# The shared expert's units leave their sequence's stage; attention writes into the sum

## The chip, the cores and the metric
The kernel runs on one core of a Trainium2 chip. The metric is the time of one execution on the device in microseconds (us), median of the runs. Engines: PE (TensorE), DVE (VectorE), ACT (ScalarE), POOL (GpSimd), SP (SyncE, which here only issues transfers). Each runs its own queue in order; the queues meet through semaphores that the code sets and waits for by hand.

## The reference, cut to what matters
Eight sequences of 512 tokens, width 512, go through attention (softmax attention and a gated linear attention over the same projections; output added to the input by the kernel, "x2"), and then through a mixture of experts:

```
shared = (silu(x @ shared_gate.T) * (x @ shared_up.T)) @ shared_down.T    # 512 -> 512 -> 512, every token
topk_idx, topk_w = _router(x, router_w, e_bias)                           # 4 of 32 experts for each token
G, U = x[slots] @ W_gate[e], x[slots] @ W_up[e]                           # 160 slots an expert, 512 -> 256
out[slots_token] += (silu(G) * U) @ W_down[e] * slots_w
result = out + shared
```

The kernel is a pre-norm block, so a layer norm stands ahead of the router and both kinds of expert, and the sum starts from x2.

## The kernel before, in words
Three phases with a barrier between them: `attention_phase` (to 2157 us of the span), `routing_phase` (L1032, to 2552 us) and `expert_phase` (L1633). Products that need more than 16 bits are made of three fp16 products of a high and a low part (`THREE`).

**Routing.** One stage for each sequence b. It holds the whole shared expert for that sequence and the routing. The shared expert has eight units: four `gate_up(b, f)` (24 matmuls of 512 columns, L1391), here called G0 to G3, and four `down(b, i, ...)` (12 such matmuls, L1398), here D0 to D3. Behind each G, ACT takes the sigmoid, DVE makes two products (`silu_product`, L1566 and L1571), ACT rounds to the high part (`h_high`, L1293), POOL subtracts the low part (`h_low`, L1202). Behind each D, DVE adds the result onto x2 (`residual`, L1579), and SP stores the sum to `acc` (L1179). PE's order in a stage: G0, `turn(b+1)` (transposes of the next sequence, L1354), `places(b)` (L1373 to L1376, prefix sums for the slots), G1, `logits(b+1)` (L1363), G2, G3, D0 to D3. DVE's order: `placing(b)`, product 0, `slots(b)` (L1553 to L1560), `statistics(b+2)`, product 1, `refine(b+2)`, `group_scores(b+1)`, `best_groups(b+1)`, product 2, `picks(b+1)`, product 3, `count_picks(b+1)`, residuals. POOL's order: `y_low(b+1)`, `copy_tokens`, then 16 scatters of 128 rows of 2112 bytes into the table `rows` (L1217) with the four `h_low` between them. `slots(b)` waits for all 16 scatters of sequence b-1 to have landed, since they read the indices that it overwrites. SP loads x2 into three buffers `xr`, and at b = 5 the weights of the first `SETS` = 5 experts.

**Experts.** One iteration for each of 32 experts. PE: `gate_up(e)` (48 matmuls of 160 columns, L1872), `turn(e+1)` (8 transposes, L1859), `down(e-1)` (12 matmuls of 512 columns, L1885). ACT and DVE split each expert's weights into high and low parts, ACT copies the result out (`copy_down`, L1785). POOL computes each slot's weight and row (`weigh`, L1726 to L1735) and adds the result to `acc` in memory with two accumulating indirect transfers of 80 rows (`add`, L1744). `add(e)` waits until `add(e-1)` has landed, as two experts may hold the same token. Results wait in four buffers `yo`. At the end SP and ACT copy `acc` to the output (L1693).

Of the kernel before, what the change touches and what calls it, by code (L numbers as in the profile page):

```python
# [6 lines left out]
P = 128  # L7
# [9 lines left out]
DM = 512  # L17
# [974 lines left out]
SETS = 5  # L992


class Held:


    def __init__(self, nc, ctx, cap):
# [7 lines left out]
        self.own = sb("own", [ct, n_ct, E_])  # L1006
        self.up_loaded = [ctx.enter_context(nc.semaphore(f"expert_up_loaded{n}")) for n in range(SETS)]
        self.down_loaded = [ctx.enter_context(nc.semaphore(f"expert_down_loaded{n}")) for n in range(SETS)]

# [14 lines left out]
def load_expert(eng, held, w_gate, w_up, w_down, e):  # L1024
# [3 lines left out]
    eng.dma_start(held.up(n), w_up[e].rearrange("(p c) i -> p c i", p=P)).then_inc(held.up_loaded[n], 16)  # L1028
    eng.dma_start(held.down(n), w_down[e].rearrange("(p c) d -> p c d", p=P)).then_inc(held.down_loaded[n], 16)


def routing_phase(nc, x2, router_w, e_bias, shared_gate, shared_up, shared_down, consts, acc_dram, rows_dram, held,  # L1032
# [10 lines left out]
    with ExitStack() as ctx:  # L1043
# [19 lines left out]
        turned_w = [[sb(f"w_t{n}_{part}", [P, 4, DM], FP16) for part in ("high", "low")] for n in range(3)]  # L1063
        sg, su, sd = turned_w
        xr = [sb(f"xr{n}", [P, NT, DM]) for n in range(RING)]
# [5 lines left out]
        y_part = [[sb(f"y{n}_{part}", [P, DC, SEQ], FP16) for part in ("high", "low")] for n in range(2)]  # L1071
# [47 lines left out]
        x_loaded = [sem(f"x_loaded{n}") for n in range(RING)]  # L1119
# [29 lines left out]
        ONE_SCATTER = 16 * NT * K  # L1149

# [3 lines left out]
        def _(sp):  # L1154
            def load_x(b):
                sp.dma_start(xr[b % RING][:], x2[b].rearrange("(i p) d -> p i d", p=P)).then_inc(x_loaded[b % RING], 16)
# [13 lines left out]
            for b in range(1, min(RING, B)):  # L1170
                load_x(b)

            for b in range(B):
                if b == max(B - 3, 0):
                    sp.wait_ge(w_ready, 12)
                    for e in range(SETS):
                        load_expert(sp, held, w_gate, w_up, w_down, e)
                sp.wait_ge(summed, NT * (b + 1))
                sp.dma_start(acc_dram[b * SEQ:(b + 1) * SEQ, :].rearrange("(i p) d -> p i d", p=P), xr[b % RING][:]).then_inc(base_stored, 16)  # L1179
                if b + RING < B:  # L1180
                    sp.wait_ge(base_stored, 16 * (b + 1))
                    load_x(b + RING)
            sp.wait_ge(base_stored, 16 * B)

        @block.gpsimd
        def _(pool):
            pool.wait_ge(loaded, ALL_LOADS)

            def y_low(b):
                for i in range(NT):  # L1190
                    t = slice(i * P, (i + 1) * P)
                    if b >= 2:
                        pool.wait_ge(up_done, SC * (b - 1))
                    pool.wait_ge(y_high_ready, NT * b + i + 1)
                    nc.gpsimd.tensor_tensor(y_part[b % 2][1][:, :, t], y_t[:, :, t], y_part[b % 2][0][:, :, t],
# [28 lines left out]
            for b in range(B):  # L1224
# [14 lines left out]
        def _(act):  # L1239
# [8 lines left out]
            def norm(b):  # L1248
                act.wait_ge(newton_step, 9 * (b + 1))
                act.wait_ge(x_loaded[b % RING], 16 * (b // RING + 1))  # L1250
# [3 lines left out]
                for i in range(NT):  # L1254
                    nc.scalar.activation(yn[b % RING][:, i, 0:DM], xr[b % RING][:, i, :], ACT.Identity,
# [14 lines left out]
            def features(b):  # L1270
                for i in range(NT):
# [6 lines left out]
                    if b >= 2:  # L1278
                        act.wait_ge(up_done, SC * (b - 1))
                    nc.scalar.activation(y_part[b % 2][0][:, :, i * P:(i + 1) * P], turned, ACT.Copy, scale=X_SCALE).then_inc(y_high_ready, 1)  # L1280
# [27 lines left out]
            if B > 1:  # L1308
                norm(1)
            for b in range(B):  # L1310
                gate_sigmoid(b, 0)
                if b + 1 < B:
                    features(b + 1)
                h_high(b, 0)
                gate_sigmoid(b, 1)
# [4 lines left out]
                h_high(b, 1)  # L1320
# [4 lines left out]
                gate_sigmoid(b, 2)  # L1325
                h_high(b, 2)
                gate_sigmoid(b, 3)
                h_high(b, 3)

        @block.tensor  # L1330
        def _(pe):
# [47 lines left out]
            def gate_up(b, f):  # L1379
# [8 lines left out]
                for w, ps, done in ((sg, gate_ps, gate_done), (su, up_ps, up_done)):  # L1388
                    for d in range(DC):
                        for n, (y_, w_) in enumerate(THREE):  # L1390
                            ins = nc.tensor.matmul(ps[f % 2][:], w[w_][:, d, f * P:(f + 1) * P], y_part[b % 2][y_][:, d, :],  # L1391
# [13 lines left out]
            pe.wait_ge(w_ready, 12)  # L1405
            for b in range(B):
                gate_up(b, 0)
# [4 lines left out]
                gate_up(b, 1)  # L1412
# [4 lines left out]
                gate_up(b, 2)  # L1417
                gate_up(b, 3)
                pe.wait_ge(h_low_ready, SC * b + 3)
                pe.wait_ge(h_step, 2 * (SC * b + 2) + 1)  # L1420
                down(b, 0, (0, 1, 2))
                pe.wait_ge(h_step, 2 * (SC * b + 3) + 1)
                down(b, 1, (0, 1, 2))
                pe.wait_ge(h_low_ready, SC * (b + 1))
                down(b, 0, (3,))
                down(b, 1, (3,))
                for i in (2, 3):
                    pe.wait_ge(summed, NT * b + i - 1)
                    down(b, i, (0, 1, 2, 3))

        @block.vector
        def _(dve):
            def statistics(b):
                base = (2 * NT + 1) * b
                dve.wait_ge(x_loaded[b % RING], 16 * (b // RING + 1))
                for i in range(NT):
                    nc.vector.bn_stats(bn[:, i, :], xr[b % RING][:, i, :]).then_inc(stats_step, 1)
# [136 lines left out]
            def residual(b, i):  # L1574
                if i == 0:
                    dve.wait_ge(x_loaded[b % RING], 16 * (b // RING + 1))
                    dve.wait_ge(yn_ready, NT * (b + 1))
                dve.wait_ge(down_done, NT * b + i + 1)
                nc.vector.scalar_tensor_tensor(out=xr[b % RING][:, i, :], in0=down_ps[i % 2][:], scalar=1.0 / (O_SCALE * W_SCALE),  # L1579
                                               in1=xr[b % RING][:, i, :], op0=ALU.mult, op1=ALU.add).then_inc(summed, 1)  # L1580
# [22 lines left out]
            for b in range(B):  # L1603
                if b:
                    placing(b)
                silu_product(b, 0)
# [7 lines left out]
                silu_product(b, 1)  # L1614
# [8 lines left out]
                silu_product(b, 2)  # L1623
                if b + 1 < B:
                    picks(b + 1)
                silu_product(b, 3)
                if b + 1 < B:
                    count_picks(b + 1)
                for i in range(NT):
                    residual(b, i)  # L1630


def expert_phase(nc, T, w, rows_dram, acc_dram, out, held):  # L1633
# [7 lines left out]
    with ExitStack() as ctx:  # L1641
# [24 lines left out]
        tr_ps, gate_ps, up_ps, down_ps = banks("tr_ps"), banks("gate_ps"), banks("up_ps"), banks("down_ps")  # L1666
# [21 lines left out]
        yo_ready = sem("yo_ready")  # L1688
        ONE_ADD = 16 * n_ct

# [8 lines left out]
        def _(sp):  # L1699
# [6 lines left out]
            for e in range(XS):  # L1706
                load_x(e)
            for e in range(XS, E_):
                if e + 1 >= SETS and e + 1 < E_:
                    sp.wait_ge(w_low, 3 * (e + 1 - SETS + 1))  # L1710
# [269 lines left out]
```

## Time and profile before
| | |
|---|---|
| median of 3 runs | 2868.56 us (2867.84 to 2871.44) |
| the profiled execution's own time | 2872.15 us |
| its span | 2869.7 us |
| PE busy | 2592.1 us, 90% |
| DVE, ACT, POOL busy | 67%, 54%, 54% |
| routing phase, by the first issues of each phase on SP | 2161 to 2552 us |
| expert phase | 2552.5 us to the end |

Busy shares are over the whole span. A matmul's record is longer than its place in the queue, since matmuls overlap: what one costs is read from start to start.

### The profile page before, as it was taken

The numbers are of one execution on the slowest core, as the hardware profiler recorded it, in microseconds if no ns is written. First come the engines' busy times: TensorE is split into PE (matmuls) and PEld (weight loads), VectorE is DVE, ScalarE is ACT, GpSimd is POOL, SyncE is SP. The second block draws the span as 40 slices with busy tenths as digits, with TensorE's granted clock in tenths as the row PEclk, the third lists the DMA queues.
The fourth block names the chain that finished last, engine by engine and source line by source line (L and its number), as shares of the span: only waits on it lengthen the run. The fifth ranks groups of instructions, "written<-read, shape, count | busy, mean of one in ns | idle before, by whom it ended". The sixth has DMA issues, their size and how long they took to land. (4 is left out here: it accounts for less than half of the span.)

```text
span 2869.7 us, 52448 instructions
## 1 busy us (share of the span) xinstructions
PE 2592.1 (90%) x16740; PEld 1703.5 (59%) x16740; DVE 1936.6 (67%) x4731; ACT 1554.0 (54%) x4655; POOL 1549.3 (54%) x1623
## 2 busy tenths in 40 slices
PE   3899999999999999999999999999984899979882
PEld 2566666666666666666666666666653444447661
DVE  5677667677776776777677767767754777747661
ACT  4566556655655555666566555656543333237661
POOL 3556445655655564566556545655520566646663
PEclk9899999999999999999999999999996999989996
DMA  4500000000000000000000000000002222339985
GB/s 169 186 1 16 1 30 1 16 30 1 1 16 31 1 16 28 3 1 16 30 1 2 15 31 1 1 31 1 1 1 107 94 69 68 132 117 272 265 231 147
DMA packets 65355, 156.78 MB, mean 55 GB/s; under 512 B 13367, under 2 KB 14647, under 8 KB 64256
## 3 DMA queue, kind: packets, MB, share of 16 engines
q1 hardware_dynamic: 48624, 132.91, 13.6%
q0 software_dynamic: 16384, 16.33, 3.1%
q10 hardware_dynamic: 80, 4.19, 0.4%
q8 instruction: 141, 2.31, 0.3%
q14 instruction: 126, 1.03, 0.1%
HBM read 120.31 MB, written 81.40 MB: 70 GB/s over the span
## 5 line engine op out<-in xcount | busy, mean ns | idle before, releaser
L403 ACT ACTIVATE prob<-score_ps,neg_max 128x512 f32<-128x512 f32 (+3 forms) x512 | 271.8, 531 | 308.1 <-DVE neg_max L566 278.6
L280 POOL TENSOR_TENSOR parts<-qk,rope 128x640 f32<-128x640 f32 x128 | 197.0, 1539 | 383.1 <-issue 326.2
L793 PE MATMUL out_ps<-prob_t,val 128*128 128x512 f32 (+3 forms) x1024 | 302.3, 438 | 14.0 <-ACT prob_t L409 13.1
L768 PE MATMUL score_ps<-kr_t,qr_t 128*128 128x512 f16 (+3 forms) x1536 | 284.7, 300 | 13.0 <-ACT prob L403 11.2
L574 DVE TENSOR_SCALAR prob<-prob,inv_sum 128x512 f32<-128x512 f32 (+3 forms) x512 | 273.7, 535 | 18.0
L793 PEld LDWEIGHTS out_ps<-prob_t,val 128*128 128x128 f32 x1024 | 185.4, 191 | 127.6 <-issue 62.1
L445 ACT ACTIVATE soft<-qk,neg_top 128x128 f32<-128x128 f32 x640 | 247.1, 387 | 5.5 <-DVE neg_top L588 2.1
L566 DVE TENSOR_REDUCE neg_max<-score_ps 128x1 f32<-128x512 f32 (+3 forms) x512 | 237.4, 483 | 7.1 <-PE score_ps L770 0.9
L309 POOL TENSOR_TENSOR decay<-keys 128x512 f32<-128x512 f32 x128 | 134.0, 1047 | 167.0 <-DVE keys L616 167.0
L835 PE MATMUL qkv_ps<-wq_high,x_t_high 128*128 128x512 f16 x512 | 195.8, 382 | 15.8 <-DVE wkv_low L514 15.8
L318 POOL TENSOR_TENSOR k_dec<-decay,keys 128x512 f32<-128x512 f32 x128 | 163.0, 1273 | 68.7 <-ACT decay L461 68.7
L572 DVE RECIPROCAL inv_sum<-row_sum 128x1 f32<-128x1 f32 x512 | 81.4, 159 | 174.6 <-ACT prob L403 174.5
L292 POOL TENSOR_TENSOR rot<-parts 128x320 f32<-128x320 f32 x128 | 110.6, 864 | 162.9 <-DVE parts L596 162.9
L835 PE MATMUL qkv_ps<-wq_low,x_t_high 128*128 128x512 f16 x512 | 195.8, 382 | 0.0
L835 PE MATMUL qkv_ps<-wq_high,x_t_low 128*128 128x512 f16 x512 | 195.3, 381 | 0.0
L331 POOL TENSOR_TENSOR o_t_low<-parts,o_t_high 128x512 f16<-128x512 f32 x128 | 147.9, 1156 | 81.0 <-ACT parts L419 81.0
L768 PEld LDWEIGHTS score_ps<-kr_t,qr_t 128*128 128x128 f16 x1536 | 135.7, 98 | 82.8 <-ACT prob L403 38.3
L889 PE MATMUL tr_ps<-q_dec,k_dec 128*32 128x128 f32 (+3 forms) x1024 | 177.6, 293 | 5.0 <-POOL k_dec L318 2.9
L298 POOL TENSOR_TENSOR soft<-soft,inv_tot 128x512 f32<-128x512 f32 x128 | 145.4, 1136 | 60.5 <-DVE inv_tot L608 60.5
L409 ACT COPY prob_t<-prob_ps 128x384 f32<-128x384 f32 (+1 forms) x256 | 94.2, 368 | 141.4 <-DVE prob_t L582 137.1
L1744 POOL DMA_INDIRECT acc<-e_yo,e_goal x64 | 113.8, 1779 | 103.5 <-issue 85.2
L1217 POOL DMA_INDIRECT rows<-r_yn,r_sk_i x128 | 129.0, 1008 | 53.9 <-issue 47.3
(267 smaller groups left out, 7701.0 us busy)
## 6 DMA issues: line engine op xcount, KB each, us to landing
held_expert_w<-in_L_ffn_W_gate_dram SPq DMA_DIRECT2D x32, 512.0 KB
held_expert_w<-in_L_ffn_W_up_dram SPq DMA_DIRECT2D x32, 512.0 KB
held_expert_w<-in_L_ffn_W_down_dram SPq DMA_DIRECT2D x32, 512.0 KB, 7.7
rows<-const_empty_dram SPq DMA_DIRECT2D x1, 10560.0 KB, 38.8
e_xg<-rows SPq DMA_DIRECT2D x32, 330.0 KB
x_in<-_attn_hidden_states_dram SPq DMA_DIRECT2D x8, 1024.0 KB, 5.5
x_acc<-_attn_hidden_states_dram SPq DMA_DIRECT2D x8, 1024.0 KB, 5.5
x<-x_acc SPq DMA_DIRECT2D x8, 1024.0 KB, 4.4
```

The lines of the kernel that those rows point to most:

```text
L280: nc.gpsimd.tensor_tensor(parts[:, 1, :].rearrange("p (h d) -> p h d", d=HALF), qk[:].rearrange("p (h d) -> p h d", d=HALF), rope[:, i, 1: ...
L298: nc.gpsimd.tensor_tensor(q, q, inv_tot[:, 0:G].unsqueeze(2).to_broadcast([P, G, DH]), ALU.mult).then_inc(soft_query_ready, 1)
L318: nc.gpsimd.tensor_tensor(k_dec[:], decay[:, 0:NSUB * P].rearrange("p (c s) -> p c s", s=P), keys[:, 0:P].unsqueeze(1).to_broadcast([P, NS ...
L331: nc.gpsimd.tensor_tensor(o_t[1][:, h, :], o_whole, o_t[0][:, h, :], ALU.subtract).then_inc(o_t_ready, 1)
L403: nc.scalar.activation(prob[:, i % 2, 0:w], score_ps[i % 2][:, 0:w], ACT.Exp, bias=neg_max[:, j:j + 1], accum_out=row_sum[:, j:j + 1]).the ...
L445: ins = nc.scalar.activation(soft[:, h * DH:(h + 1) * DH], qk[:, h * DH:(h + 1) * DH], ACT.Exp, bias=neg_top[:, h:h + 1], accum_out=tot[:, ...
L566: nc.vector.tensor_reduce(neg_max[:, j:j + 1], score_ps[i % 2][:, 0:w], AX_X, ALU.max, negate=True).then_inc(max_ready, 1)
L574: nc.vector.tensor_scalar(prob[:, i % 2, 0:w], prob[:, i % 2, 0:w], inv_sum[:, j:j + 1], None, ALU.mult).then_inc(prob_ready, 1)
L768: nc.tensor.matmul(score_ps[i % 2][:, 0:w], qr_t[p][:, q_, h, i * P:(i + 1) * P], kr_t[p][:, k_, 0:w], start=(n == 0), stop=False)
L793: nc.tensor.matmul(out_ps[:, j * P:SEQ], val[p][:, j, :], prob_t[:, j, j * P:SEQ], start=(j == 0), stop=False, skip_group_check=True)
L835: ins = nc.tensor.matmul(qkv_ps[:, 0:G * DH], x_t[x_part][:, d, i * P:(i + 1) * P], wq[w][:, d, gn * G * DH:(gn + 1) * G * DH], start=(d = ...
L889: ins = nc.tensor.matmul(tr_ps[0][0:m, :].rearrange("p (h t) -> p h t", t=P)[:, :, m - SUB:m], k_dec[:, s, 0:m], q_dec[:, :, m - SUB:m], s ...
```

## The change
- The 64 units of the shared expert form one row, sequence after sequence. The first five sequences' 40 units are done during routing, five in each of the eight stages (`place`), whatever sequence they belong to. The remaining 24 units (three sequences: 12 G, 12 D) are done between the experts (`late_pieces`): one unit ahead of `gate_up(e)` in experts 0, 1, 2, 4, 5, 6, 8 and so on to 30, none in every fourth expert.
- To that end the normalised sequences stay in five buffers (`Y_RING`) and the shared weights stay in SBUF; preloaded expert weights go down from five sets to four; `xr` from three buffers to two. A separate buffer `x_sum` with its own loads serves the five early sequences.
- Attention writes x2 into the rows of `acc` itself. So the three late sequences need no base: their unit results are added to `acc` by four accumulating indirect transfers of 128 rows per sequence on POOL (`s_add`), with a wait for the adds before and a wait of the next `add` for them.
- Expert phase: `gate_ps` and `up_ps` go from two banks to one each (two banks go to the late units), the order of ACT, DVE and POOL within an iteration changes, weights are loaded in two steps.

```diff
-SETS = 5
+SETS = 4
+EARLY = 5
+PIECES = 2 * 4
+Y_RING = 5
...
+        IN_STAGE = EARLY * PIECES // B
+        def place(b, n):
+            q = IN_STAGE * b + n
+            return q // PIECES, q % PIECES
...
-                h_low(b, 0)
-                scatter(b, range(0, 3))
-                h_low(b, 1)
-                scatter(b, range(3, 9))
-                h_low(b, 2)
-                scatter(b, range(9, 10))
-                h_low(b, 3)
-                scatter(b, range(10, NT * K))
+                for n, some in enumerate((range(0, 3), range(3, 8), range(8, 10), range(10, 12), range(12, NT * K))):
+                    q, part = place(b, n)
+                    if part < SC:
+                        h_low(q, part)
+                    scatter(b, some)
...
+            def piece(b, n):
+                q, part = place(b, n)
+                if part < SC:
+                    gate_up(q, part)
+                else:
+                    i = part - SC
+                    pe.wait_ge(h_low_ready, SC * (q + 1))
+                    if i >= 2:
+                        pe.wait_ge(summed, NT * q + i - 1)
+                    down(q, i, range(SC))
...
+            def s_add(q, experts):
+                pool.wait_ge(added, ONE_ADD * experts)
+                pool.wait_ge(s_out_ready, NT * (q + 1))
+                for i in range(NT):
+                    n = NT * (EARLY + q) + i
+                    pool.indirect_dma_start(acc_dram, bass.IndirectOffsetOnAxis(ap=held.token_i[:, n:n + 1], axis=0), s_out[:, i, :], None,
                                            bounds_check=T + cap - 1, oob_is_err=True, compute_op=ALU.add).then_inc(s_added, 16)
...
             for e in range(E_):
-                if e + 2 < E_:
-                    weigh(e + 2)
-                add(e)
+                for q, part in late_pieces(e):
+                    if part < SC:
+                        s_low(q, part)
+                if e:
+                    if e + 1 < E_:
+                        weigh(e + 1)
+                    add(e - 1)
+                for q, part in late_pieces(e):
+                    if part == PIECES - 1:
+                        s_add(q, e)
+            add(E_ - 1)
...
-                if e >= 2:
-                    pe.wait_ge(h_step, 2 * (e - 1))
+                if e:
+                    pe.wait_ge(h_step, 2 * e)
...
-            turn(0)
             for e in range(E_):
+                for q, part in late_pieces(e):
+                    s_piece(q, part)
+                if not e:
+                    turn(0)
                 gate_up(e)
...
-    x2 = scratch("x2", [B, SEQ, DM])
-    acc = scratch("acc", [B * SEQ + cap, DM])
+    acc = scratch("acc", [T + cap, DM])
+    x2 = acc[0:T, :].rearrange("(b t) d -> b t d", b=B)
```

## Rows read from the trace of the kernel before
**Rows 1.** Windows: length, busy us (instructions) of each engine, granted clock, DMA share, GB/s
```profile
2300.00:2400.00 100.00, 94.49 (x515) 48.72 (x513) 70.27 (x177) 34.72 (x61) 63.28 (x62) 0.98 0.22 72
2700.00:2800.00 100.00, 83.60 (x779) 65.97 (x777) 67.57 (x95) 64.35 (x107) 61.78 (x94) 0.98 0.87 239
```
**Rows 2.** Timeline, PE, one routing stage: start, duration, instruction
```profile
2352.99 0.27 PE L1354 MATMUL r_tr_ps<-held_ident,r_yn 128*128 128x128 f32 x1
2356.31 0.18 PE L1373 MATMUL r_pos_ps<-r_picked_b,r_before_b 128*128 128x32 bf16 x1
2356.66 0.38 PE L1391 MATMUL r_gate_ps<-r_y_high,r_w_t_high 128*128 128x512 f16 x1
2361.84 0.19 PE L1363 MATMUL r_lg_ps<-r_rw_t,r_y_t 128*128 128x32 f32 x1
2365.69 0.61 PE L1391 MATMUL r_gate_ps<-r_y_high,r_w_t_high 128*128 128x512 f16 x1
...
2377.36 0.38 PE L1398 MATMUL r_gate_ps<-r_w_t_high,r_h_high 128*128 128x512 f16 x1
2388.13 0.38 PE L1391 MATMUL r_gate_ps<-r_y_high,r_w_t_high 128*128 128x512 f16 x1
```
**Rows 3.** Timeline, DVE, the same stage
```profile
2356.85 0.29 DVE L1553 TENSOR_SCALAR r_over<-r_pos_ps 128x128 f32<-128x128 f32 x1 [2.91 <-PE r_pos_ps L1376]
...
2372.52 0.69 DVE L1566 TENSOR_TENSOR r_sig<-r_sig,r_gate_ps 128x512 f32<-128x512 f32 x1
...
2377.63 0.69 DVE L1566 TENSOR_TENSOR r_sig<-r_sig,r_gate_ps 128x512 f32<-128x512 f32 x1
...
2378.95 1.05 DVE L1525 TENSOR_REDUCE r_picked<-r_hot 128x128 f32<-128x512 f32 x1
...
2381.61 0.19 DVE L1473 TENSOR_TENSOR r_seen<-r_seen,r_seen_now 128x32 f32<-128x32 f32 x1
```
**Rows 4.** Timeline, DVE: one cast, for sequences 1 and 4
```profile
2248.45 0.23 DVE L1516 CAST r_at_f<-r_at 128x32 f32<-128x32 uint32 x1
...
2375.13 1.74 DVE L1516 CAST r_at_f<-r_at 128x32 f32<-128x32 uint32 x1
```
**Rows 5.** Timeline, DVE and POOL: `slots(1)`, its first and last scatter, first of sequence 7
```profile
2276.59 0.29 DVE L1553 TENSOR_SCALAR r_over<-r_pos_ps 128x128 f32<-128x128 f32 x1 [2.91 <-PE r_pos_ps L1376]
...
2281.76 1.02 POOL L1217 DMA_INDIRECT rows<-r_yn,r_sk_i  x1 [0.90 <-DVE r_sk_i L1560]
...
2307.29 0.97 POOL L1217 DMA_INDIRECT rows<-r_yn,r_sk_i  x1 [0.31 <-issue]
...
2516.98 1.00 POOL L1217 DMA_INDIRECT rows<-r_yn,r_sk_i  x1 [0.90 <-DVE r_sk_i L1560]
```
**Rows 6.** Timeline, SP: first transfers of the expert phase
```profile
2552.46 1.80 SPq L1704 DMA_DIRECT2D e_xg<-rows  x4
```
**Rows 7.** Timeline, PE, and a window: D units of sequence 7 after a wait
```profile
2533.23 0.61 PE L1398 MATMUL r_gate_ps<-r_w_t_high,r_h_high 128*128 128x512 f16 x1 [4.51 <-POOL r_h_low L1202]
...
2530.00:2540.00 10.00, 6.77 (x19) 2.53 (x20) 0.00 (x0) 0.15 (x1) 8.40 (x9) 0.66 0.03 4
```
**Rows 8.** Timeline, PE: first matmuls of two experts early in the phase
```profile
2580.28 0.23 PE L1872 MATMUL e_gate_ps<-e_xp_t_high,e_wg_high 128*128 128x160 f16 x1
...
2587.16 0.23 PE L1872 MATMUL e_gate_ps<-e_xp_t_high,e_wg_high 128*128 128x160 f16 x1
```
**Rows 9.** View of line L1744: all adds, then landing from issue
```profile
L1744 POOL DMA_INDIRECT acc<-e_yo,e_goal x64: 1414/1708/2516, 2575.2 to 2838.1; - x64
...
DMA to landing us min/median/max: 3.9/5.9/8.8
```
**Rows 10.** Timeline, POOL and SP: last adds and the copy to the output
```profile
2836.34 1.41 POOL L1744 DMA_INDIRECT acc<-e_yo,e_goal  x1 [3.30 <-issue]
2838.06 1.42 POOL L1744 DMA_INDIRECT acc<-e_yo,e_goal  x1 [0.30 <-issue]
...
2842.00 0.55 SPq L1693 DMA_DIRECT2D out_dram<-acc  x1
```

More of the change, by code:

```diff
@@ L1070, in routing_phase @@
         y_t = sb("y_t", [P, DC, SEQ])
-        y_part = [[sb(f"y{n}_{part}", [P, DC, SEQ], FP16) for part in ("high", "low")] for n in range(2)]
+        y_part = held.y_part
+        x_sum = sb("x_sum", [P, NT, DM])
         bn = sb("bn", [P, NT, 6])
@@ L1118, in routing_phase @@
         w_ready = sem("w_ready")
-        x_loaded = [sem(f"x_loaded{n}") for n in range(RING)]
+        x_loaded = [sem(f"x_loaded{n}") for n in range(2)]
+        x_sum_loaded = sem("x_sum_loaded")
         gate_done = sem("gate_done")
@@ L1324, in _ @@
                     norm(b + 2)
[L1325 to L1328, printed above, removed]
+                for n in range(2, IN_STAGE):
+                    sigmoid_of(b, n)
+                    high_of(b, n)
         @block.tensor
@@ L1416, in _ @@
                     logits(b + 1)
[L1417 to L1429, printed above, removed]
+                for n in range(2, IN_STAGE):
+                    piece(b, n)
         @block.vector
@@ L1572, in silu_product, with residual, piece @@
                                                in1=up_ps[f % 2][:], op0=ALU.mult, op1=ALU.mult).then_inc(h_step, 1)
-            def residual(b, i):
+            def residual(q, i):
                 if i == 0:
[L1576 to L1580, printed above, removed]
+                    dve.wait_ge(x_sum_loaded, 16 * (q + 1))
+                dve.wait_ge(down_done, NT * q + i + 1)
+                nc.vector.scalar_tensor_tensor(out=x_sum[:, i, :], in0=down_ps[i % 2][:], scalar=1.0 / (O_SCALE * W_SCALE),
+                                               in1=x_sum[:, i, :], op0=ALU.mult, op1=ALU.add).then_inc(summed, 1)
+            def piece(b, n):
+                q, part = place(b, n)
+                if part < SC:
+                    silu_product(q, part)
+                else:
+                    residual(q, part - SC)
             statistics(0)
@@ L1622, in _ @@
                     best_groups(b + 1)
[L1623 removed]
+                piece(b, 2)
                 if b + 1 < B:
                     picks(b + 1)
[L1626 removed]
+                piece(b, 3)
                 if b + 1 < B:
                     count_picks(b + 1)
[L1629 to L1630 removed]
+                for n in range(4, IN_STAGE):
+                    piece(b, n)
 def expert_phase(nc, T, w, rows_dram, acc_dram, out, held):
@@ L1665, in expert_phase @@
         h_part = [[sb(f"h{n}_{part}", [P, FC, cap], FP16) for part in ("high", "low")] for n in range(2)]
-        tr_ps, gate_ps, up_ps, down_ps = banks("tr_ps"), banks("gate_ps"), banks("up_ps"), banks("down_ps")
+        tr_ps, down_ps = banks("tr_ps"), banks("down_ps")
+        gate_ps, up_ps, wide_ps, wider_ps = (ctx.enter_context(nc.psum_tensor(f"e_{name}", [P, 512], F32))
+                                            for name in ("gate_ps", "up_ps", "wide_ps", "wider_ps"))
+        s_sig = sb("s_sig", [P, SEQ])
+        s_h = sb("s_h", [P, SEQ])
+        s_part = [sb(f"s_{part}", [P, SC, SEQ], FP16) for part in ("high", "low")]
+        s_out = sb("s_out", [P, NT, DM])
+        sg, su, sd = held.shared_w
         def by_chunk(bank):
```

233 lines of the change are left out of this document (180 added, 53 removed).

## The prediction
> **What bounds the kernel now.** I read the windows by stretch first. In routing PE is busy 94 of 100 us with DMA at 0.22; among the experts PE has 84 of 100 and DMA 0.87 [rows 1]. So the two phases have different limits, and the change moves PE work from the one where PE is full to the one where it isn't.
>
> In routing the timeline of PE shows a stage of 40.1 us without gaps (first scatter of sequence 1 to that of sequence 7: 2516.98 - 2281.76 = 235.2 us, six stages, of which the last is shorter, 34.2; the other five take 40.1 to 40.3) [rows 5]. From start to start a G costs 5.2 us (2356.66 to 2361.84), four D cost 10.8 (2377.36 to 2388.13), so 2.7 each, the transposes 3.3, the places 0.35, the logits 3.85 [rows 2]. 4 x 5.2 + 10.8 + 7.5 = 39.1; a wait of 1.2 us inside G2 makes up the rest. PE sets the stage.
>
> Among the experts PE takes 6.9 us for one when nothing holds it (2580.28 to 2587.16) [rows 8], but 64 adds in 32 pairs start from 2575.2 to 2838.1, 263 / 31.5 = 8.3 us a pair [rows 9]. A pair needs 1.7 us from the first issue to the second, and then the landing, for which the next pair waits: 4.7 us at the quiet end (3.30 idle + 1.42), median 5.9 [rows 9, 10]. 1.7 + 5.9 and the hand-over are some 8 us: the chain of adds on POOL sets this phase, and PE loses 1.4 us an expert.
>
> **Routing after the change.** Its PE work per stage falls from 39.1 to (20 x 5.2 + 20 x 2.7) / 8 + 7.5 = 27.2 us. By that alone the eight stages would give back 95 us. They can't: another chain lies close below. `slots(b)` on DVE waits for all scatters of b-1. From its start S to the first scatter it is 5.2 us (2276.59 to 2281.76); sixteen scatters stand 1.28 us apart (with four `h_low` between them 25.5 us from first to last: 15 x 1.28 + 3 x 1.2 and two short waits) [rows 5]; then the last must land. For the landing of a scatter no row exists. The nearest are the adds: 3.9 us at the least, 5.9 median, from the issue [rows 9]. A plain write should not be slower than a read and write; I take 4.0, with 2.5 and 5.9 as ends. So POOL's chain without waits is 5.2 + 19.2 + 4.0 = 28.4 us, and 1.3 for each `h_low` between.
>
> The second limit is DVE's order. From S: to the end of `best_groups` 15.7 us with a G product inside (2356.85 to 2372.52), 15.0 with a residual (0.7 for 1.3); then unit 2 and `picks` 5.1 (4.5 with a residual; 2372.52 to 2377.63), unit 3 1.3 or 0.7, `count_picks` 2.85 (2378.95 to 2381.8), unit 4 [rows 3]. If unit 4 is a G, its product ends at S + 24 to 26, then ACT's rounding and POOL's `h_low` take 2.0, and only then come the last four scatters (3.85) and the landing. The stages, with their five units:
> - stage 0 (G G G G D): starts as before; its D0 waits for the fourth `h_low` at 2257 (three scatters more than before stand ahead of it, but only one D follows, not four). `slots(1)` at 2268.9, against 2276.6: 7.7 earlier.
> - stage 1 (D D D G G): unit 4 ends at 24.9; + 2.0 + 3.85 + 4.0 = 34.7.
> - stage 2 (G G D D D): 28.4 + 2.1 for an `h_low` that waits = 30.5.
> - stage 3 (D G G G G): unit 4 at 26.3, `h_low` at 28.3; PE's D0 of the same sequence waits for it, then transposes and places: + 4.9 + 3.7 = 37.0.
> - stage 4 (D D D D G): 24.2 + 2.0 + 7.85 = 34.0, and 1 more as the experts' weights load just then.
> - stage 5 (G G G D D): D0 waits for G3's `h_low` at 19.1; D0, D1, D2 (4.9 + 2.6 + 2.6), transposes and places 3.8 = 33.1.
> - stage 6 (D D G G G): no `statistics`; POOL 28.4 + 3 x 1.3 and hand-overs = 32.8.
> The D behind a wait is taken at 4.9, not 2.7: a D after 4.5 us of waiting starts at 0.61 us a matmul, and the window has a granted clock of 0.66, so partly 1.2 and not 2.4 GHz [rows 7].
> From stages 1 and 4 I take off 2.0 and 2.5: DVE's cast took 1.74 us where an `h_low` ran on POOL beside it and 0.23 where none did [rows 4], and these stages have fewer `h_low` in that place. Sum: 32.7 + 30.5 + 37.0 + 32.5 + 33.1 + 32.8 = 198.6, so `slots(7)` at 2467.5. Sixteen scatters, landing and barrier, 28.3 more: the expert phase starts at 2495.8, where it started at 2552.5 [rows 6]. **Gain 56.7 us.** (Bounds: with landings of 5.9 us the five stages that end on one and the phase's end give 11 back; with 2.5, 9 more are gained.)
>
> SP's new waits cost nothing: the loads of x2 for the norm and of `x_sum` are issued at least 5 us ahead of their reader in each stage by the same chain; the latest is sequence 7's, issued at the end of stage 4, needed 13 us later. If that cover were gone, each late load would cost its 5.6 us once. Preloading four sets instead of five is hidden too: the fifth is asked for as soon as expert 0's weights are split, four experts ahead. In attention the stores go to other addresses, the same number: nothing.
>
> **Experts after the change.** Here PE becomes the limit: 6.9 us an expert and 12 x 5.2 + 12 x 2.6 = 93.3 us for the late units, 314 in all, against 8.3 x 32 = 266 for the adds. Step by step from the phase's start: G0 cold takes 7.6 and hides the first loads, transposes and the split of x 2.3 (the first `gate_up` at 10.2); 31 iterations at 6.88, less the missing first `down`, 210.7; the other 23 units 88.1. PE ends iteration 30 at 309.0. ACT and DVE need some 6 us an expert plus 1.3 for a G, below PE's 6.9 plus 5.2; the single banks `gate_ps` and `up_ps` are free 0.7 us after `gate_up`, while PE transposes and runs `down` (3.6 us): nothing. If that cover went, each us would cost 31.
> `s_add` lengthens POOL's chain three times. An accumulating transfer of 128 rows isn't in the trace; by the 80-row ones (1.42 us and 0.3 between) four of them and a landing are 3 x 1.72 + 4.7 = 9.9; scaled with the rows 13.7; I take 11.5. The first two are absorbed: POOL needs 8 us an expert, PE 9.8 on average, and the four `yo` buffers hold the lag for the six experts in which it is caught up. The third lies in the last iteration, ahead of the last two adds: 0.9 + 6.5 (add 29) + 11.5 + 6.5 + 5.7 (1.7 + 3.9) = 31.1 [rows 10]. Then the copy to the output, 27.7 (2842.0 to 2869.7) [rows 10]. 309.0 + 31.1 + 27.7 = 367.8, against 317.2 before. **Loss 50.6 us** (bounds: 48 to 58 by the transfer's size and a cold or warm start).
>
> **Sum.** Span 2495.8 + 367.8 = 2863.6, 6.1 less than 2869.7. The profiled execution took 2872.15, 3.6 above the median of the runs; on the median the forecast is 2868.56 - 6.1 = 2862.5 us. Two sums of 50 us nearly cancel: PE's idle time in the experts was only 1.4 x 32 = 45 us, and half of it comes back as the tail.
>
> The Trainium skill (TensorE: Matmul & The Clock Gate, Part 1, "What's actually happening") says that the slow clock is the default state and activity releases it. That agrees with the window at 0.66 [rows 7], and speaks against the change, as routing now has PE waits in each stage: it is the first rival. The skill (DMA: Bandwidth & Descriptors, "Anatomy of one DMA") gives a transfer a fixed 2.0 us plus its bytes at 436 GB/s; for 270 KB that is an estimate of 2.6 us, near my lower end, and by it routing would gain 8 us more. No row shows it; a case near it is rival 3.
>
> **Rivals.**
> 1. *Routing waits cost more than I took.* PE waits 5 to 10 us in each stage and starts slow, not only in two: 2.5 us in each of four more, and scatters land in 5.9: 10 + 11 = 21, so the net is +15, 2883; with half of it 2873. For it: rows 7. Against: in most stages PE isn't last, so a slow start is hidden. It decides when PE's transposes end later than the landing.
> 2. *The adds' chain isn't absorbed (the other side).* If POOL lags beyond the four buffers after each `s_add`, or the loaded landing of the 128-row transfers is longer, ACT's `copy_down` holds PE's `down`: 2 x 11.5 = 23 more, net +17, 2885. For it: this very chain sets the phase now. Against: it must lag about 20 us before it reaches PE, and one `s_add` is 11.5.
> 3. *Routing goes better:* landings of 2.5 us and fewer stretched DVE operations in all stages, 2 us each: 9 + 8 = 17 more, 2846.
> 4. *The stage doesn't shorten* since DVE and POOL were as full as PE: then +50 - 10. Against: DVE has 70 of 100, POOL 63 [rows 1], and the sums above.
>
> **Chances.** My forecast with its own range of 2852 to 2870: 0.45 (of it faster 0.25, within 0.16, slower 0.04). Rival 1: 0.18 (slower 0.14, within 0.04). Rival 2: 0.13 (slower 0.12, within 0.01). Rival 3: 0.19, faster. Rival 4: 0.05, slower. About 0.2% (5.7 us) is what a measurement of this kernel can tell from no change. Faster 0.44, within 0.21, slower 0.35. The range 2846 to 2883 leaves out the far end of rivals 2 and 4.
>
> **What will show it.** First scatters of the sequences 30 to 37 us apart, with the longest behind the stage with four G; the experts' first loads near 2496 (over 2505: rival 1; under 2485: rival 3). Among the experts PE busy over 95 of 100, without waits for `e_xp_t_low`, DMA under 0.87; PE's `down` waiting for `e_yo` would be rival 2. The last add some 31 us behind PE's last but one expert. The forecast is wrong if the routing phase gains under 45 us or the expert phase loses over 60.

## The result and the profile after

The changed kernel takes 2881.6 us (median; 2878.5 to 2884.9) beside 2871.4 us of the kernel before in the same session, a ratio of 1.0037 (95% interval 1.0023 to 1.0052). It is 10 us slower; the forecast was 6 us faster. The profiled execution took 2881.60 us, and its span is 2879.7 us, 10.0 more than before.

First the rows of the page that answer to the table of before: the engines' busy times, the granted clock and the DMA share in 40 slices.

```profile
span 2879.7 us, 52505 instructions
...
PE 2596.8 (90%) x16740; PEld 1708.1 (59%) x16740; DVE 1921.5 (67%) x4719; ACT 1571.3 (55%) x4667; POOL 1580.5 (55%) x1636
...
PE   3899999999999999999999999999985788799892
...
PEclk9899999999999999999999999999996989899996
DMA  4500000000000000000000000000003314288876
```

PE's busy time is the same (2592.1 before), as the same work is done. To see where time went I cut the span at two issues on SP: the first load of routing (2163.82, before 2161.24) and the first load of the experts:

```profile
2494.10 1.32 SPq L1786 DMA_DIRECT2D e_xg<-rows  x3
```

Routing takes 330.3 us where it took 391.2 [rows 6], 60.9 less. The expert phase takes 385.6 (2879.7 - 2494.1) where it took 317.2, 68.4 more. Attention ends 2.6 later. 68.4 + 2.6 - 60.9 = 10.1. The forecast had 56.7 less and 50.6 more: routing was right within 4.2 us, and the expert phase was forecast 17.8 us too short.

The windows of the changed kernel, with the columns of rows 1: one in routing, one in the quiet middle of the expert phase, one behind it.

```profile
2300.00:2400.00 100.00, 82.55 (x453) 44.51 (x452) 73.34 (x220) 38.67 (x67) 72.51 (x72) 0.90 0.24 81
2620.00:2720.00 100.00, 100.00 (x826) 70.82 (x825) 64.58 (x89) 65.23 (x102) 67.24 (x85) 1.00 0.84 233
2720.00:2780.00 60.00, 48.15 (x377) 34.35 (x376) 28.75 (x38) 27.59 (x44) 38.16 (x47) 0.89 0.70 181
```

PE fell from 94 to 83 of 100 us in routing, and its granted clock from 0.98 to 0.90. In the expert phase it is busy, but for 1 us, from its first matmul up to 2727, as forecast. Then a hole opens. The view of waits of PE over the expert phase has three rows (total, times, longest), the first of which is the end of routing:

```profile
PE e_wide_ps L2052 <- PEq L1054: 16.9, 1, 16.9
PE e_gate_ps L2024 <- DVE e_xp_t_low L1949: 10.4, 2, 9.3
PE e_wide_ps L2063 <- POOL e_s_low L1843: 2.5, 1, 2.5
```

To find what stands behind the 9.3 us I read the timelines of the engines ahead of PE, each row with its idle time and releaser. PE waits for DVE's low part of x. But DVE itself had waited, and so had ACT, whose rounding of x comes behind its rounding of the late product (`s_high`):

```profile
2736.61 0.31 PE L2024 MATMUL e_gate_ps<-e_xp_t_high,e_wg_high 128*128 128x160 f16 x1 [9.34 <-DVE e_xp_t_low L1949]
```
```profile
2732.53 0.62 ACT L1912 CAST e_s_high<-e_s_h 128x512 f16<-128x512 f32 x1 [14.09 <-DVE e_s_h L1979]
```
```profile
2731.81 0.69 DVE L1979 SCALAR_TENSOR_TENSOR e_s_h<-e_s_sig,e_wider_ps 128x512 f32<-128x512 f32 x1 [11.87 <-POOL e_s_low L1843]
```

DVE can't write the next late G into the one buffer `s_h` before POOL has subtracted the low part (`s_low`) of the last. And POOL stands in `s_add`:

```profile
2712.28 2.47 POOL L1835 DMA_INDIRECT acc<-e_yo,e_goal  x1 [2.14 <-issue]
...
2723.33 1.58 POOL L1850 DMA_INDIRECT acc<-e_s_out,held_token_i  x1 [6.86 <-DMA acc<-e_yo,e_goal]
...
2728.93 1.55 POOL L1850 DMA_INDIRECT acc<-e_s_out,held_token_i  x1 [0.30 <-issue]
2729.94 1.73 POOL L1843 TENSOR_TENSOR e_s_low<-e_s_h,e_s_high 128x512 f16<-128x512 f32 x1
...
2735.53 1.59 POOL L1835 DMA_INDIRECT acc<-e_yo,e_goal  x1 [2.36 <-DMA acc<-e_s_out,held_token_i]
```

From the add before the second `s_add` to the add behind it, 23.3 us pass (2712.28 to 2735.53); the three steps ahead of it are 9.7, 8.6 and 7.9. The four instructions of `s_add` take 7.2 us to issue (2723.33 to 2730.48), and `s_low` comes behind them. Its input has been ready since 2709.8, where ACT's `s_high` ends, so only its place in the queue makes it wait.

PE feels the second `s_add` and not the first. Two things differ. Behind the first, expert 11, where the second G of the next sequence could stand, has no late unit, so that G comes an expert later; behind the second `s_add` it comes at once, in expert 22. And POOL was later: this is read from how far an expert's add starts behind the end of PE's product for it. Here are the last matmuls of two products; their adds are those at 2712.28 and 2735.53 above:

```profile
2702.77 0.38 PE L2037 MATMUL e_down_ps<-e_wd_high,e_h_low 128*80 128x512 f16 x1
...
2714.84 0.38 PE L2037 MATMUL e_down_ps<-e_wd_high,e_h_low 128*80 128x512 f16 x1
```

The distance goes from 9.1 to 20.3 us. Ahead of the first `s_add` it was 1.6; that one made it 14.1, and ten experts later it was still 9.1. So the second met a POOL that had not caught up with the first. Without these 7.5 us (9.1 - 1.6) PE's wait of 9.34 would be about 2, as an estimate.

PE has lost 9.34 + 2.51 us in waits, and 2.6 + 1.6 in the slow starts behind them (the gate and up products of that expert take 5.9 us instead of 3.3, at a granted clock of 0.62 from 2736 to 2744; the D behind the other wait 4.2 instead of 2.6, at 0.72 from 2772 to 2778). That is 16.1 of the 17.8 us. PE ends its last but one expert at +325.3 from the phase's start (2819.39), where +309.0 was forecast. The rest is in the tail: 32.2 us up to the copy instead of 31.1, and 28.1 for the copy instead of 27.7.

### The profile page after: what moved, and what is told of

Read it like the earlier page. It is cut to its first block and busy times, and to the rows that moved or that the text cites. A ratio compares the mean times of both kernels' runs of the same rounds, so it can differ in the third digit from the quotient of the medians.

```text
span 2879.7 us, 52505 instructions
## 1 busy us (share of the span) xinstructions
PE 2596.8 (90%) x16740; PEld 1708.1 (59%) x16740; DVE 1921.5 (67%) x4719; ACT 1571.3 (55%) x4667; POOL 1580.5 (55%) x1636
## 5 line engine op out<-in xcount | busy, mean ns | idle before, releaser
L793 PE MATMUL out_ps<-prob_t,val 128*128 128x512 f32 (+3 forms) x1024 | 302.4, 439 | 14.0 <-ACT prob_t L409 13.1
```

The source lines that it names most:

```text
L793: nc.tensor.matmul(out_ps[:, j * P:SEQ], val[p][:, j, :], prob_t[:, j, j * P:SEQ], start=(j == 0), stop=False, skip_group_check=True)
```

## The experiments

Each is compared with the kernel before on the same chip. Lengths of the phases are from one profiled execution of each kernel, which isn't always near the median: for e2 it took 2874.0 us, for e10 2886.5, for e11 2861.5.

| kernel | median us | ratio to before, interval | routing | experts |
|---|---|---|---|---|
| changed kernel | 2881.6 | 1.0037 [1.0023, 1.0052] | 330.3 | 385.6 |
| e1: two `s_h` | 2881.2 | 1.0031 [1.0020, 1.0041] | 330.3 | 386.2 |
| e2: `s_add` one turn later | 2879.9 | 1.0030 [1.0019, 1.0041] | 326.9 | 382.3 |
| e3: no `s_add` | 2849.5 | 0.9924 [0.9908, 0.9939] | 327.3 | 356.6 |
| e4: before, x2 in the sum | 2871.7 | 0.9997 [0.9989, 1.0006] | 388.2 | 317.4 |
| e8: `s_low` on DVE | 2870.5 | 0.9997 [0.9985, 1.0009] | 328.1 | 377.8 |
| e5: no late units | 2821.0 | 0.9826 [0.9804, 0.9848] | 326.8 | 326.1 |
| e13: e5 with two banks | 2818.3 | 0.9808 [0.9794, 0.9822] | 328.2 | 327.1 |
| e9: e8, six early | 2871.8 | 1.0002 [0.9991, 1.0014] | 348.7 | 357.3 |
| e10: e9, late units in front | 2871.5 | 1.0002 [0.9985, 1.0020] | 352.1 | 367.1 |
| e11: sum at the end | 2856.1 | 0.9933 [0.9920, 0.9946] | 330.3 | 362.2 |
| e12: e11, six early | 2854.0 | 0.9927 [0.9914, 0.9940] | 350.8 | 336.2 |

The kernels with the changed routing and five early sequences have 326.8 to 330.3 us of routing, so differences of 3 us between single profiles mean nothing.

**e1, two buffers for the late product.** The first theory blamed the single buffer.

```diff
-        s_h = sb("s_h", [P, SEQ])
+        s_h = [sb(f"s_h{n}", [P, SEQ]) for n in range(2)]
...
-                if m:
-                    dve.wait_ge(s_low_ready, m)
-                nc.vector.scalar_tensor_tensor(out=s_h[:], ...
+                if m >= 2:
+                    dve.wait_ge(s_low_ready, m - 1)
+                nc.vector.scalar_tensor_tensor(out=s_h[m % 2][:], ...
```

> The changed kernel with two s_h buffers instead of one: DVE's product of a late G waits for the s_low before the last, no longer for the last. Theory A (the stall of PE at 2727 to 2737 and at 2770 comes from s_low standing behind s_add(1) on POOL, which the single s_h hands to DVE, ACT and the split of x): the waits of 9.34 and 2.51 us and the slow starts behind them (2.6 and 1.6) go, 16 us less, 2865 to 2868 us median, expert phase 370. DVE's wait of 11.87 us for s_low is gone, but the s_low itself is still late: D0 of that sequence comes four units later, so nobody misses it. Rival B (the lag of the chain of adds behind s_add is what PE pays, through copy_down and yo or through the x split): the wait moves to another name and the time stays at 2879 to 2882. Rival C (the miss is in the routing or attention phase): no change either, and the expert phase stays 385.

Measured: 2881.2 us, no gain to be told from the changed kernel, and an expert phase of 386.2. PE's waits in it:

```profile
...
PE e_wide_ps L2063 <- POOL e_s_low L1843: 13.5, 1, 13.5
PE e_gate_ps L2024 <- DVE e_xp_t_low L1949: 1.1, 1, 1.1
```

The wait of 9.34 us has gone and one of 13.5 has come, three experts later, at the next sequence's D0, which needs all four `s_low`. So theory A fell: the buffer chooses the place of the stall and not its size. POOL is late, and whatever PE needs from it next shows that. This is rival B, but with `s_low` as the path, not `yo`.

**e2, `s_add` one turn later.**

```diff
-                for q, part in late_pieces(e):
-                    if part == PIECES - 1:
-                        s_add(q, e)
+                for o in (e - 1, e):
+                    for q, part in late_pieces(o):
+                        if part == PIECES - 1 and (o < e) == (o < 30):
+                            s_add(q, e)
...
```

> The changed kernel with the first two s_add moved one turn of POOL's loop later, so that the s_low of the next sequence's G0 stands ahead of s_add(1) and not behind it; the one s_h stays. Theory A (s_low behind s_add): the stall goes, 12 to 16 us less, 2866 to 2870. The next G1's s_low (one expert later) may now stand behind s_add(1) and leave up to 4 us of it. Rival B (the length of POOL's chain, wherever s_add stands): no change, 2880 to 2882, with the stall one expert later.

Measured: 2879.9, ratio 1.0030; again at most 2 us, where theory A wanted 12 to 16. PE's longest wait is for the same `s_low`, at D0:

```profile
...
PE e_wide_ps L2064 <- POOL e_s_low L1843: 9.7, 1, 9.7
PE e_gate_ps L2025 <- DVE e_xp_t_low L1950: 2.1, 2, 1.1
```

Rival B again: it is the lag of POOL's queue, not the place of one instruction in it.

**e3, no `s_add`.** The late results are computed and left out of the sum.

```diff
-                for q, part in late_pieces(e):
-                    if part == PIECES - 1:
-                        s_add(q, e)
...
```

> The changed kernel without any s_add: the three late sequences' shared results are computed and not added to the sum. Theory A: the whole stall goes (16 us) and the tail loses the third s_add (11.9 us by the profile after): 28 less, 2853 us, expert phase 357. If s_add cost only its tail (rival B, the stall has another cause): 12 less, 2870, and PE still waits about 9 us for e_xp_t_low near expert 21.

Measured: the expert phase is 356.6 us, 29.0 less than in the changed kernel (28 expected); the ratio went from 1.0037 to 0.9924, that is 32 us. PE has no wait in the phase over 1.1 us and ends its last but one expert at +307.6. The `s_add` calls cause the whole stall and 11 us of the tail (49.0 us behind that end instead of 60.3).

**e4, one part of the change alone: x2 in the rows of the sum.**

```diff
-    x2 = scratch("x2", [B, SEQ, DM])
-    acc = scratch("acc", [B * SEQ + cap, DM])
+    acc = scratch("acc", [T + cap, DM])
+    x2 = acc[0:T, :].rearrange("(b t) d -> b t d", b=B)
```

> The kernel before with one part of the change alone: attention writes x2 into the rows of the sum, everything else as it was. Theory A (same stores, other addresses): ratio 1.000, the first routing load at 2161 us. Rival (the phase of attention is 2.6 us longer in the changed kernel because of the place of its stores): 2.6 us more, 2874 on a median of 2871.4, first routing load at 2164.

Measured: 0.9997, first routing load at 2160.76. The stores' new place costs nothing. The 2.6 us by which attention ended later in the changed kernel's profile are chance: that load stands anywhere from 2160.65 to 2166.78 in the profiles of the kernels here.

**e8, `s_low` on DVE.** This cuts the path by which POOL's lag reached PE and leaves the lag.

```diff
...
                 down_low(e)
+                for q, part in late_pieces(e):
+                    if part < SC:
+                        s_low(q, part)        # now nc.vector.tensor_tensor
                 if e + 1 < E_:
                     x_low(e + 1)
```

> The changed kernel with the subtraction s_low of the late G units moved from POOL to DVE (behind the split of the third weight), one s_h as before: nothing that PE needs for a late unit stands behind an s_add any more. Theory A2 (POOL's lag behind s_add reaches PE only through s_low, wherever the buffer lets it out: 13.5 us of it in the run with two s_h): the waits of PE in the expert phase go, expert phase 385.6 - 16 - about 1 (twelve s_low of 1.66 us less in POOL's chain matter only in the tail) = 369, the ratio to before 0.998, 2867. Rival B2 (the lag reaches PE also through the slots' shares of `weigh`, for which ACT's copy_down already waited 3 us in that run, or through yo): PE then waits for e_yo instead, 8 to 12 us, and the ratio stays at 1.002 or more.

Measured: ratio 0.9997, 11 us better than the changed kernel by the ratios, about 8 by the phase's length, and level with the kernel before. The window where the hole was, and the waits of PE over the whole expert phase:

```profile
2720.00:2780.00 60.00, 60.00 (x496) 42.64 (x495) 39.45 (x59) 40.31 (x64) 37.11 (x49) 1.00 0.81 216
```
```profile
...
PE e_gate_ps L2024 <- DVE e_xp_t_low L1939: 1.1, 1, 1.1
```

PE now ends its last but one expert at 2797.61, +308.9: the 309.0 of the forecast. So the path was `s_low`. But the phase is 377.8 long and not 369. The missing 9 us are in the tail, in POOL's timeline:

```profile
2807.27 1.49 POOL L1835 DMA_INDIRECT acc<-e_yo,e_goal  x1 [1.74 <-issue]
...
2813.69 1.58 POOL L1843 DMA_INDIRECT acc<-e_s_out,held_token_i  x1 [3.21 <-DMA acc<-e_yo,e_goal]
...
2825.86 1.41 POOL L1835 DMA_INDIRECT acc<-e_yo,e_goal  x1 [5.03 <-DMA acc<-e_s_out,held_token_i]
...
2832.29 1.42 POOL L1835 DMA_INDIRECT acc<-e_yo,e_goal  x1 [3.30 <-issue]
```

The add of expert 29 starts at 2807.27, 9.7 us behind PE's product for it, where in the changed kernel it starts 1.6 behind (2821.01 against 2819.39). POOL hasn't caught up by the end: its distance behind PE was 1.6 us ahead of the first `s_add` and 14.3 behind it, 9.1 ahead of the second and 22.7 behind it, and 9.7 here. The adds' chain sets the end of the phase, with PE's waits gone. Half of the stall that was removed came back as lag in the tail.

**e5 and e13, no late units; and then two banks again.** Both leave the shared expert of the last three sequences out of the result. e5 gives the routing gain alone; e13 tests the forecast's "nothing" for the single banks.

```diff
-            return [(n // PIECES, n % PIECES) for n in range(3 * (e + 1) // 4, 3 * (e + 2) // 4) if n < LATE]
+            return []
...
```
```diff
...
-                for w_part, ps, done in ((wg_part, gate_ps, gate_done), (wu_part, up_ps, up_done)):
+                for w_part, ps, done in ((wg_part, (gate_ps, wide_ps)[e % 2], gate_done), (wu_part, (up_ps, wider_ps)[e % 2], up_done)):
```

> The changed kernel without any late unit in the expert phase: the shared part of the last three sequences is left out, routing is as in the changed kernel. It gives the routing gain alone. If the two phases are independent (theory): routing 330, expert phase set by the chain of adds again at 8.3 us an expert, 317; together 61 less than before, 2812, ratio 0.979. If the new order on POOL and ACT or the four sets of weights cost something by themselves (rival): expert phase 322 or longer, 2817 and more.

> The kernel without late units (the last three sequences' shared part left out) with two PSUM banks each for the experts' gate and up products again, as in the kernel before. The run without late units had an expert phase of 326.1 us against 317.2 before, with adds 8.7 us apart and not 8.4, and PE waiting 38.6 us for the low part of x. Theory D (memory traffic and the new order of loads): no change, 326. Rival E (the single banks cost something when PE isn't the limit): 317 to 320, 6 to 9 us less than the 2821 of that run.

Measured: e5 has 326.8 us of routing and 326.1 of experts, 2821.0 in all. Routing is as long as with late units, so the two phases are independent; the expert phase is 9 us longer than before, the rival's side (2817 and more) and not the theory's 2812. Nearly all of it lies between the first add and the last: 31 steps of 8.7 us instead of 8.4. e13 has 327.1 by its profile, so the banks don't make the 9 us; its ratio is 0.0018 lower than that of e5, with intervals that overlap. What does make them stays open. In e5's middle window the DMA share is higher than in rows 1 at the same bytes, which fits adds that come some 9.5 us apart there, but isn't shown as the cause:

```profile
2620.00:2720.00 100.00, 80.06 (x738) 65.26 (x739) 58.83 (x86) 59.07 (x96) 55.41 (x88) 0.95 0.95 239
```

**e9 and e10, six sequences early.** Both on the basis of e8.

```diff
-EARLY = 5
+EARLY = 6
...
+            return [divmod(e // 2, PIECES)] if e % 2 == 0 else []            # e9
+            n = e // 3 * 2 + e % 3                                           # e10
+            return [divmod(n, PIECES)] if e % 3 < 2 and n < LATE else []
```

> As the kernel with s_low on DVE, with six sequences early instead of five: six units a routing stage (two scatters behind the sixth), 16 late units, one in every second expert. PE's work among the experts falls by 8 units of 3.9 us = 31, one s_add is gone; POOL's chain (32 x 8.3 + 2 x 12) then is as long as PE's. Expert phase 340 to 348 with the tail; routing: PE's work per stage 31.2 us, a stage 33 to 36 instead of 30.5 to 37, +10 in all. Forecast 2850, ratio 0.992. If routing stages were bound by PE alone after all, +24 there and 2864.

> As the one before, but the 16 late units stand in two of every three experts and end at expert 22, so that the last s_add isn't in the tail. If PE and POOL's chain of adds overlap as theory A2 says, the tail loses 11.9 us and POOL's chain sets the end: 8 to 12 less than the one before, 2840. If s_add's lag in the middle is not caught up (rival B2) or the last ten experts then run at the chain's 8.3 us with PE idle, as the chain is the limit over the whole phase, the gain is 0 to 4.

Measured: both level with the kernel before, so both forecasts (2850 and 2840) were missed. In e9 routing is 20.6 us longer than in e8, nearer to the 24 of a stage bound by PE than to my 10: `slots` waits for PE in six of the seven stages, where in the changed kernel it is three. The expert phase is 20.5 shorter, and not 30 to 38. PE ends its last but one expert at +284.8, as summed in the expectation of e12 (285), but the add of expert 29 starts 13.1 us behind: the lag of the one `s_add` in the middle isn't gained back. The share moved is paid one to one. e10's median is the same; its profiled run is its longest, so the 367.1 is not to be compared. It shows that the path that rival 2 of the prediction named (PE's `down` behind ACT's `yo`) does exist, where late units stand closer:

```profile
PE e_gate_ps L2025 <- DVE e_xp_t_low L1940: 12.4, 10, 2.6
PE e_down_ps L2038 <- ACT e_yo L1890: 12.3, 2, 10.9
```

**e11 and e12, a version without `s_add`.** e3 left the late results out of the sum; here they come into it at no cost for POOL.

```diff
+            load_rest(sp, 0)              # rows of the sum -> SBUF, behind the last add
+            load_rest(sp, 2)
             copy_half(sp, 0)              # now the first five sequences only
+            store_rest(sp, 0)
+            store_rest(sp, 2)
...
+                for i in range(NT):       # DVE, at the end
+                    part = rest(q)[:, i:i + 1, :]
+                    nc.vector.tensor_tensor(part, part, s_out(q, i), ALU.add).then_inc(rest_summed, 1)
```

> A version meant to beat both: the changed kernel with no s_add. The three late sequences' shared results stay in SBUF (the first in s_out, the other two in two y buffers that are free by then); when the last add has landed, those sequences' rows of the sum are loaded, DVE adds the results, and they are stored to the output, while the other five sequences are copied as before. Theory: POOL carries 32 adds only, PE sets the phase as in the run without s_add (356.6 us, ratio 0.9924), and the end costs the load, the add and the store instead of a part of the copy: the same bytes, one transfer latency and one DVE add more, 3 to 8 us. Forecast 2856, ratio 0.9945. If the route through SBUF is slower than the copy from memory to memory (rival): 12 us or more at the end, ratio 0.997 or higher.

> The same with six sequences early and two late (one late unit in every second expert). Routing as measured with six units a stage, 349 to 352 us. Expert phase: PE needs 285 to its last but one expert, the chain of adds without s_add 28 + 31 x 8.3 + 34 = 320. If the adds' chain is the limit there (theory): 320 + 350 = 670 against 684 for the three-late version, 12 us less than that one, 2843. If instead the memory traffic of the phase is (DMA share 1.0 in the windows of the six-early run, rival): 330 + 350, no gain over it, 2854.

Measured: e11 has 2856.1 us (2856 forecast), ratio 0.9933, by the ratios 30 us faster than the changed kernel and 19 faster than the kernel before. Behind the last add the end takes 33.0 us (first load issued at 2826.31, span 2859.3) instead of 28.1: 4.9 more, within the 3 to 8 expected. e12 has 0.9927, 2854.0 us: no difference from e11 that can be told, as its rival forecast (2854), and not the theory's 2843. Its expert phase is 26 us shorter, its routing 20.5 longer. That phase came out at 336 and not 320, but the rival's reason, memory traffic, isn't shown by it. The adds up to that of expert 29 start 1.6 to 3.5 us behind PE's products, so the chain keeps up and PE sets the pace; PE ends its last but one expert at +283.3, and the tail with the route through SBUF takes 52.9. My sum compared PE's 285 without its tail with the chain's 320 with it. The middle window has PE full, and that at a DMA share of 0.95 (in e9's it is 0.95 too, not the 1.0 of my expectation):

```profile
2620.00:2720.00 100.00, 100.00 (x871) 74.35 (x869) 67.62 (x97) 71.20 (x112) 68.90 (x94) 1.00 0.95 257
```

## Why the prediction was wrong

**Routing was forecast rightly.** Routing was bound by PE, and taking PE's work out of it was to give back 56.7 us (60.9 measured). The first scatters of the sequences came 29.6 to 34.9 us apart (forecast 30 to 37), with the longest behind the stage with four G. That the total came out so well is in part luck. From one `slots` to the next the six stages took 32.2, 32.5, 33.3, 35.4, 30.7 and 30.6 us, where I had 32.7, 30.5, 37.0, 32.5, 33.1 and 32.8: they miss by up to 3.7 us, to both sides. The last scatter's landing, for which I took 4.0 with 2.5 and 5.9 as ends, shows as 2.2 to 6.4 us from its issue to the `slots` that waits for it:

```profile
2302.41 0.29 DVE L1595 TENSOR_SCALAR r_over<-r_pos_ps 128x128 f32<-128x128 f32 x1 [5.69 <-DMA rows<-r_yn,r_sk_i]
...
2403.61 0.29 DVE L1595 TENSOR_SCALAR r_over<-r_pos_ps 128x128 f32<-128x128 f32 x1 [7.24 <-DMA rows<-r_yn,r_sk_i]
...
2464.91 0.29 DVE L1595 TENSOR_SCALAR r_over<-r_pos_ps 128x128 f32<-128x128 f32 x1 [3.02 <-DMA rows<-r_yn,r_sk_i]
```

(The last scatters ahead of them start at 2298.80, 2397.19 and 2462.68.) Rival 1 is out. PE did wait 3.6 to 6.1 us in five of the stages, where I had two, and the clock did fall to 0.90. But of the seven `slots` behind the first only three waited for PE (`r_pos_ps`), and the other four for a scatter: there a slow PE is hidden. One reading of mine was wrong, without effect on the sum: the 1.2 us "wait inside G2" of the kernel before is none. The first matmuls behind the logits start 0.41 to 0.43 us apart instead of 0.22, at a granted clock of 0.50 from 2365 to 2368.

**PE's sum in the expert phase was right.** The first `gate_up` came at +10.1 (10.2), and without the stall PE ends at +308.9 (309.0; run e8) or +307.6 (e3). The tail was right within 1.1 us and its `s_add` measured 11.9 us (2827.52 to 2839.40) for 11.5. The moved base and the single banks cost nothing that shows (e4, e13), nor do SP's new waits: no engine waited for a load of `x_sum`.

**The step that failed** is this sentence: "The first two are absorbed: POOL needs 8 us an expert, PE 9.8 on average, and the four `yo` buffers hold the lag for the six experts in which it is caught up." Two things are wrong in it.
- *The path.* I asked who waits for POOL's adds and found `yo`. I did not ask what else stands in POOL's queue. `s_low` stands there, between the adds, and PE needs it about one expert later, by way of `s_h`, DVE and ACT. Its slack is one expert, not four. Moving it to DVE takes the stall away (e8); two buffers or another place of `s_add` in POOL's order don't (e1, e2).
- *The size.* The quiet `s_add` at the end is 11.9 us, but the two in the middle stretch the step between the adds around them from PE's 9.8 us to 24.5 (2598.04 to 2622.55) and 23.3. Each puts POOL 11 to 14 us further behind PE (in e8 from 1.6 to 14.3 and from 9.1 to 22.7). One of the two landings beside each is longer than in the tail: 11.9 us from the last issue of the first to the add behind it, where the tail has 6.3, and 11.1 us from the add at 2712.28 to the second, where the tail has 6.5. The traffic beside them (DMA share 0.84 from 2620 to 2720) may be the reason; no run shows that. And POOL gains the lag back at 0.5 us an expert behind the first, and in e8 at 1.4 behind the second, so six experts are not enough: 7.5 us of the first are left when the second comes, and in e8 8 us are left at the end.

The forecast called itself wrong if the expert phase lost over 60 us; it lost 68.4. Rival 2 had the right side and nearly the right price (2885 against 2881.6 measured), and named this very chain; it got 0.13, because I tested it against the wrong buffer. That its price is so near is in part luck: it was 23 us by way of `yo`, and what came is 16 by way of `s_low` and 1.5 in the tail, with routing 4 better than forecast and attention 2.6 later. The Trainium skill (DMA: Bandwidth & Descriptors, "Rules for kernel authors") says that an accumulating transfer must wait for an earlier one on the same bytes, else an addition is lost. The kernel keeps to that: its trace has 12.8 us of waits of adds for the landings of `s_add`, in three places. No run here left such a wait out, so what would be lost without it isn't shown. As long as the late results are added by such transfers, each late sequence puts one more landing into the chain.

**The gain was given back, not lost.** In e9 and e12 one sequence more or less among the experts moves 20 to 26 us from one phase to the other. The kernel before had 45 us of idle PE in the expert phase [rows 8, 9], with the chain of adds as the limit. The late units filled PE, and their `s_add` at the same time lengthened that chain. The units alone did no harm to it: without `s_add` the adds up to that of expert 29 start 1.6 to 2.9 us behind their products (e3).

## What to carry to other kernels

When work is put behind a queue's long instruction, list everything else that this queue holds and the slack of each reader: the lag comes out at the shortest slack, and a second buffer or another place in the same queue only moves it. A serial chain that sets a phase must not be lengthened to fill another engine's holes; take the added link out of the chain instead (here by adding the late results once, at the end, at 4.9 us, where `s_add` took 29). A link of accumulating transfers costs its issue plus the landings on both sides, and in the middle of this phase these took up to 11.9 us, where the quiet rows of the tail have 6.3 to 6.5. And reckon whether a lag is caught up before the next one comes: here the second met 7.5 us of the first.

## What the runs showed of the hardware

An accumulating indirect transfer of 128 rows of 2 KB holds POOL for 1.55 to 2.23 us, hardly more than one of 80 rows (1.41 to 2.47), by these rows (shortest, median and longest in ns):

```profile
L1850 POOL DMA_INDIRECT acc<-e_s_out,held_token_i x12: 1546/1556/2230, 2605.1 to 2833.1; - x12
L1835 POOL DMA_INDIRECT acc<-e_yo,e_goal x64: 1407/1496/2466, 2522.4 to 2847.7; - x64
```

From issue to landing the 128-row transfers took 4.6 to 10.9 us, median 5.3, the 80-row ones 3.9 to 9.0, median 5.3:

```profile
DMA to landing us min/median/max: 4.6/5.3/10.9
...
DMA to landing us min/median/max: 3.9/5.3/9.0
```

PE was slow without a wait ahead of it, too. In the kernel before, the 512-column matmuls right behind the logits (matmuls of 32 columns, with no idle time between them and these) started 0.41 to 0.43 us apart at a granted clock of 0.50 (2365 to 2368), and 0.22 apart 3 us later.

A route through SBUF with an addition on the way (three sequences loaded, added and stored while the other five are copied from memory to memory) took 33.0 us where the plain copy of all eight takes 28.1.
